# A graph and expert network on one core: the three expert layers split the 626 node columns as 250 + 376, and the steps that use the routing come one up product later

## The reference

```python
xf = layernorm(x)                                   # 625 x 768
probs = softmax(xf @ gate_w.T)                      # 625 x 8 experts
top_w, top_i = top_k(probs, 2)
top_w = top_w / (top_w.sum(-1) + 1e-9)
combine = zeros(625, 8); combine[t, top_i] += top_w
h = gelu(einsum('td,edh->teh', xf, w1) + b1)        # 8 experts of 192 (f0, f3) or 128 (f1)
y = einsum('teh,ehd->ted', h, w2) + b2
x = x + einsum('ted,te->td', y, combine)
```

## Time and profile before

| | |
|---|---|
| three runs | 1741.81, 1742.04, 1739.98 us; median 1741.81 |
| the profiled execution | 1739.98 us; its span from first to last instruction 1740.0 us |
| PE busy | 1682.7 us (97%), 10227 matmuls |
| DVE, POOL, ACT busy | 54%, 40%, 27% of the span |
| chain of work that ended last | PE 82%, DVE 11%, ACT 4% |
| f0: first router matmul, cT transposes | 258.85 us, 279.44 us |
| f1: the same | 514.22 us, 535.98 us |
| f3: the same | 1598.73 us, 1620.90 us |

### The profile page before, as it was taken

How to read it: one execution, slowest core, us unless ns; L and a number is a source line. 1 busy time by engine, 2 the same in 40 slices (tenths; PEclk the granted TensorE clock), 3 DMA queues, 4 the chain that set the end, 5 groups by cost and what they waited for, 6 DMA issues and landing times.

```text
span 1740.0 us, 25810 instructions
## 1 busy us (share of the span) xinstructions
PE 1682.7 (97%) x10227; PEld 1579.9 (91%) x10227; DVE 931.1 (54%) x1879; ACT 466.8 (27%) x875; POOL 690.3 (40%) x428
## 2 busy tenths in 40 slices
PE   8799999999999988899999999999999999999999
PEld 7699999997999988799377888989999999998999
DVE  8993537416866679857497554423112141225731
ACT  6443123203223138934222211101011011112310
POOL 1026865652445520060020175431644435342663
PEclk9899999999999999899899999999999999999999
DMA  2002222423212210014010022111221111110222
GB/s 90 1 28 70 73 69 65 142 78 128 64 55 64 64 56 10 1 47 143 7 43 1 11 85 64 57 45 37 73 64 55 46 51 59 55 55 30 64 73 72
DMA packets 42000, 99.84 MB, mean 57 GB/s; under 512 B 10509, under 2 KB 12143, under 8 KB 41895
## 3 DMA queue, kind: packets, MB, share of 16 engines
q1 hardware_dynamic: 37828, 87.87, 16.3%
q10 hardware_dynamic: 4066, 10.46, 1.7%
HBM read 96.39 MB, written 1.92 MB: 57 GB/s over the span
## 4 chain that ended last, share of the span: by engine, by line
PE 82%; DVE 11%; ACT 4%; issue 1%; POOL 1%; DVEq 0%; POOLq 0%; ACTq 0%
PE bank L2421 10%; PE bank L2423 10%; PE bank L2422 10%; PE banks L2421 9%; PE banks L2422 9%; PE banks L2423 9%; PE bank L2983 3%; PE banks L2983 3%; PE bank L3060 3%; PE bank L3065 3%; PE banks L3060 2%; PE banks L3065 2%; DVE tmp L1827 1%; DVE src_hot L1491 1%; PE banks L2835 1%
## 5 line engine op out<-in xcount | busy, mean ns | idle before, releaser
L833 POOL TENSOR_TENSOR w_hi<-raw,ones_r 128x768 fp32r<-128x768 f32 (+1 forms) x192 | 294.0, 1532 | 994.9 <-PE banks L2423 368.3
L836 POOL TENSOR_TENSOR w_lo<-raw,w_hi 128x768 fp32r<-128x768 f32 (+1 forms) x192 | 370.5, 1930 | 15.0
L2421 PE MATMUL bank<-w_hi,xT_hi 128*125 128x384 f32 (+2 forms) x560 | 187.8, 335 | 1.7 <-DVE small L1968 1.2
L2423 PE MATMUL bank<-w_hi,xT_lo 128*125 128x384 f32 (+2 forms) x560 | 186.7, 333 | 0.0
L2422 PE MATMUL bank<-w_lo,xT_hi 128*125 128x384 f32 (+2 forms) x560 | 186.5, 333 | 0.0
L2421 PE MATMUL banks<-w_hi,xT_hi 128*125 128x384 f32 (+2 forms) x440 | 151.8, 345 | 0.2 <-DVE xT_lo L1569 0.2
L2422 PE MATMUL banks<-w_lo,xT_hi 128*125 128x384 f32 (+2 forms) x440 | 151.4, 344 | 0.0
L2423 PE MATMUL banks<-w_hi,xT_lo 128*125 128x384 f32 (+2 forms) x440 | 151.3, 344 | 0.0
L1618 DVE TENSOR_TENSOR hT_lo<-tmp,hT_hi 128x312 fp32r<-128x312 f32 (+1 forms) x88 | 94.3, 1078 | 41.9 <-ACT hT_hi L970 41.5
L2421 PEld LDWEIGHTS bank<-w_hi,xT_hi 128*125 128x125 f32 x560 | 103.9, 186 | 5.0 <-DVE small L1968 1.4
L2422 PEld LDWEIGHTS bank<-w_lo,xT_hi 128*125 128x125 f32 x560 | 103.9, 185 | 2.5
(11 more groups left out here) (579 smaller groups left out, 3923.4 us busy)
## 6 DMA issues: line engine op xcount, KB each, us to landing
raw<-wa SPq DMA_DIRECT2D x92, 384.0 KB, 3.0
raw<-wc SPq DMA_DIRECT2D x76, 384.0 KB, 3.0
raw<-wb SPq DMA_DIRECT2D x28, 448.0 KB, 3.3
w_rows<-w_in ACTq DMA_DIRECT2D x1, 3072.0 KB, 12.6
bias<-bias_in ACTq DMA_DIRECT2D x6, 384.0 KB
w_first<-w_in ACTq DMA_DIRECT2D x1, 2304.0 KB, 11.2
w_down<-w_down_in SPq DMA_DIRECT2D x8, 288.0 KB, 5.2
w_up<-w_up_in SPq DMA_DIRECT2D x1, 2304.0 KB, 10.6
```

Source lines behind the costliest of these rows:

```text
L833: pool.tensor_tensor(w_hi[:, k, 0:width], raw[:, k, 0:width], ones[:, 0:1].to_broadcast([P, width]), ALU.mult).then_inc(S("unit_high"), 1)
L836: pool.tensor_tensor(w_lo[:, k, 0:width], raw[:, k, 0:width], f(w_hi[:, k, 0:width]), ALU.subtract).then_inc(S("unit_split"), 1)
L2421: tell_used(pe.matmul(dst, l_hi, r_hi, start=start, stop=False))
L2423: return pe.matmul(dst, l_lo, r_hi, start=False, stop=stop)
```

## The change

The expert layers get column parts of their own, 250 (tiles 0 and 1) and 376 (tiles 2 to 4 and the pad). `router(0)` waits for the first two tiles only. The last tile's turn moves behind job 0, `router(1)` behind job 1, the router's transposes behind job 2, the importance of f1 behind job 5, the wait for `combine` with the transposes of the experts' weights behind job 6, and the spreading starts behind job 7. The first four jobs change their order from (unit, part) = (0,0) (0,1) (1,0) (1,1) to (0,0) (1,0) (0,1) (1,1). The slots of `tmp` are five of 376 columns in the same memory, plus two in memory that is free at that time, so seven in all. The down products wait for at least four `low`. The order of the bank plan (`plan_groups`) follows the same steps.

```diff
+EXPERT_CH = [(0, 2 * TN), (2 * TN, NP - 2 * TN)]
...
-EXPERT_LAG = 6
-IMPORTANCE = 3
+EXPERT_LAG = 7
+IMPORTANCE = 5
+EXPERT_SLOTS = 7
+ROUTER_JOB = 1
...
     if s == "g0" and j < 6:
         return j % 3, j // 3
+    if s != "g0" and j < 4:
+        return j % 2, j // 2
     return j // 2, j % 2
+
+
+def columns_of(s, c):
+
+    return (CH if s == "g0" else EXPERT_CH)[c]
...
         add(f + "_routerT", 0, f + "_routerT_read", 1)
-        left_turn()
         jobs, lag = 2 * tiles, EXPERT_LAG
         for j, spread in enumerate(spread_after(jobs)):
             if j < jobs:
                 add(f + "_hidden", j, f + "_activated", j + 1)
             if j == 0:
+                left_turn()
+            if j == ROUTER_JOB:
                 add(f + "_routerT", 1, f + "_routerT_read", 2)
-            if j == 1:
+            if j == ROUTER_JOB + 1:
                 add(f + "_router", 0, f + "_routed", 1)
...
+        last_slots = {s: [at_(f"{s}_slot{i}", [P, EXPERT_CH[1][1]], f32, off)
+                          for i, off in enumerate((XT + up32(KD * NP * 4), HT + 8 * NP * 4 if s == "f1" else NM + 20480))]
+                      for s in ("f0", "f1", "f3")}
...
+        expert_tmp = at_("expert_tmp", [P, TSLOTS - 1, EXPERT_CH[1][1]], f32, tmp_off)
...
+        def slot_of(s, j, cn):
+
+            if s == "g0":
+                return tmp[:, j % TSLOTS, 0:cn]
+            k = j % EXPERT_SLOTS
+            return expert_tmp[:, k, 0:cn] if k < TSLOTS - 1 else last_slots[s][k - TSLOTS + 1][:, 0:cn]
...
                 def router(c):
-                    c0, cn = CH[c]
-                    pe.wait_ge(*E(s + "_xT_low", (6, 2 * NT)[c]))
+                    c0, cn = EXPERT_CH[c]
+                    pe.wait_ge(*E(s + "_xT_low", (4, 2 * NT)[c]))
...
                 router(0)
-                turn_behind(s)(NT - 1)
                 jobs = 2 * tiles
                 for j, spread in enumerate(spread_after(jobs)):
                     if j < jobs:
                         up(s, j)
                     if j == 0:
+                        turn_behind(s)(NT - 1)
+                    if j == ROUTER_JOB:
                         router(1)
-                    if j == 1:
+                    if j == ROUTER_JOB + 1:
                         pe.wait_ge(*E(s + "_routerT_read", 2))
...
-                down(s + "d", s + "_down", hT_hi, hT_lo, lambda k: pe.wait_ge(*E(s + "_low", 2 * k + 2)), seed=seed,
+                down(s + "d", s + "_down", hT_hi, hT_lo, lambda k: pe.wait_ge(*E(s + "_low", max(2 * k + 2, 4))), seed=seed,
```

More of the change, by code:

```diff
@@ L593, in network @@
         tmp = at_("tmp", [P, TSLOTS, WIDE], f32, tmp_off)
+        expert_tmp = at_("expert_tmp", [P, TSLOTS - 1, EXPERT_CH[1][1]], f32, tmp_off)
+        assert (TSLOTS - 1) * EXPERT_CH[1][1] <= TSLOTS * WIDE
         iota = new("iota", [TN, NP], i16)
@@ L962, in hidden @@
                 weighted = full == s + "_weighted"
+                slots = EXPERT_SLOTS if weighted else TSLOTS
                 steps = spread_after(jobs) if weighted else [range(max(j - TSLOTS + 1, 0), max(j - TSLOTS + 2, 0))
@@ L967, in high @@
                     m, c = job_of(s, i)
-                    c0, cn = CH[c]
+                    c0, cn = columns_of(s, c)
                     act.wait_ge(*E(full, i + 1))
-                    act.activation(hT_hi[:, m, c0:c0 + cn], tmp[:, i % TSLOTS, 0:cn], ACT.Copy
+                    act.activation(hT_hi[:, m, c0:c0 + cn], slot_of(s, i, cn), ACT.Copy
                                    ).then_inc(S(s + "_high"), 1)
@@ L976, in hidden @@
                         m, c = job_of(s, j)
-                        cn = CH[c][1]
-                        if made <= j - TSLOTS:
+                        cn = columns_of(s, c)[1]
+                        if made <= j - slots:
                             high(made)
@@ L981, in hidden @@
                         await_group(act, s + "_hidden", j)
-                        if j >= TSLOTS:
-                            act.wait_ge(*E(s + "_low", j - TSLOTS + 1))
-                        act.activation(tmp[:, j % TSLOTS, 0:cn], bank(s + "_hidden", j)[:, 0:cn], func,
+                        if j >= slots:
+                            act.wait_ge(*E(s + "_low", j - slots + 1))
+                        act.activation(slot_of(s, j, cn), bank(s + "_hidden", j)[:, 0:cn], func,
                                        **scale_bias(m)).then_inc(S(s + "_activated"), 1)
@@ L992, in expert_layer @@
                 normal_rows(s)
-                for c, (c0, cn) in enumerate(CH):
+                for c, (c0, cn) in enumerate(EXPERT_CH):
                     await_group(act, s + "_routerT", c)
@@ L1607, in hidden_low @@
                     if j < jobs and weigh:
-                        cn = CH[j % 2][1]
+                        cn = columns_of(s, job_of(s, j)[1])[1]
                         dve.wait_ge(*E(s + "_activated", j + 1))
                         await_group(dve, s + "_cB", j)
-                        TT(tmp[:, j % TSLOTS, 0:cn], tmp[:, j % TSLOTS, 0:cn], bank(s + "_cB", j)[:, 0:cn], ALU.mult
+                        TT(slot_of(s, j, cn), slot_of(s, j, cn), bank(s + "_cB", j)[:, 0:cn], ALU.mult
                            ).then_inc(S(s + "_weighted"), 1)
@@ L1615, in hidden_low @@
                         m, c = job_of(s, i)
-                        c0, cn = CH[c]
+                        c0, cn = columns_of(s, c)
                         dve.wait_ge(*E(s + "_high", i + 1))
-                        TT(hT_lo[:, m, c0:c0 + cn], tmp[:, i % TSLOTS, 0:cn], f(hT_hi[:, m, c0:c0 + cn]),
+                        TT(hT_lo[:, m, c0:c0 + cn], slot_of(s, i, cn), f(hT_hi[:, m, c0:c0 + cn]),
                            ALU.subtract).then_inc(S(s + "_low"), 1)
@@ L2613, in expert_layer @@
                     for i in spread:
-                        m, (c0, cn) = i // 2, CH[i % 2]
+                        m, c = job_of(s, i)
+                        c0, cn = columns_of(s, c)
                         q, kind = (m // 3, m % 3) if tiles == 12 else (m // 2, 2 * (m % 2))
```

## The result

The changed kernel takes 1747.74 us (median of 6 runs, 1746.93 to 1749.9), the kernel before beside it 1742.13 (6 runs): a ratio of 1.0034, 95% interval 1.0024 to 1.0044, so 0.34% slower. The forecast was 1743.7 with a range up to 1747.5; it is missed by 4.0 us, and the range by 0.2.

The account below looks back on a forecast made before the run. PE, busy 97% of the span, was taken as the bound. Earlier router starts (-5.8 us) against new routing stalls (+2.5, +2.7, +2.5) gave +1.9 us on the median 1741.81: 1743.7 us, range 1738.5 to 1747.5.

Parts of the forecast that it names:

- The widths: Expert-layer matmuls: 250 columns cost 0.116 to 0.117 us, 376 cost 0.172, together as before; value 0, +-1.2 us.
- no penalty for narrow ones: Rival for the expert matmuls: narrow ones run at the plain float32 form's rate, +190 us, about 1930 us; chance 0.04.
- The handover: First router matmul starts earlier, f3's last turn waits 0.5 us; gains f0 1.0, f1 0.85, f3 4.0, sum 5.8 us.
- The routing chain: DVE's routing, slowed by POOL, makes PE wait at the experts' weights: 2.5 us in f0 and f3, 2.7 in f1.
- R + 12.8: DVE's chain in f0 and f3 ends 12.8 us after the job behind the router's transposes starts; PE comes at 10.4.
- both comparisons are held: In DVE's routing, POOL delays two comparisons, to 5.3 and 7.2 us after the job behind the router's transposes starts.
- Sum: Net of gains and stalls in the three expert layers: f0 +1.5, f1 +1.85, f3 -1.5, together +1.9 us.
- I count the clock as kept: At f3's router, idle shrinks from 2.7 to 0.5 us, so the lower clock goes away: 1.6 us gained.
- The stalls bring the lower clock: Rival: one to three clock falls behind the new stalls, 1.6 us each, giving 1745.3 to 1748.6 us; chance 0.24.
- idle there with a fall of the clock behind it: Sign of being wrong: PE idle at the experts' weight transposes (L2608), followed by the lower clock.
- the matmuls around the stalls are dense: Argument against clock falls at the new stalls: matmuls there are dense, those before f3's router were short transposes.
- 2.1 us of cover: One more job before PE asks for combine; four jobs, 10.4 us, still lie between in f0, as before.

Follow-up runs that it names:

- e1: Changed kernel, but POOL starts the second weight unit given back behind the router's numbers only after the copies into cpad, in all three expert layers; 1738.7 us, 0.9978 of before.
- e3: Changed kernel, but PE fills its wait for cpad in each expert layer with 14 thrown-away products of 376 columns; 1743.34 us, 1.0011 of before.
- e9: Changed kernel with lag 8 and eight slots, plus ten thrown-away products (1.7 us) ahead of f1's transposes of the experts' weights; 1733.84 us, 0.9959 of before.
- e12: Changed kernel with lag 8 and eight slots, plus five thrown-away products (0.9 us) ahead of f1's transposes of the experts' weights; 1737.61 us, 0.9966 of before.
- e8: Changed kernel with the lag left at 6 and six slots, so new parts and order alone; 1742.90 us, 1.0005 of before.
- e11: Changed kernel (lag 7), but POOL holds back only the third weight unit until cpad is made; 1737.99 us, 0.9973 of before.
- e10: Changed kernel with lag 6, six slots, importance behind up product 4, and POOL holding the second weight unit until cpad is made; 1737.76 us, 0.9976 of before.
- e2: Changed kernel with every step that uses the routing one up product later (lag 8, eight slots); 1737.3 us, 0.9974 of before.
- e4: Changed kernel with even column parts (312 and 314) again and the first router product waiting for six copies as before; 1755.83 us, 1.0082 of before.

## Why the prediction was wrong

**What held.** The widths: products of 250 columns start 0.117 us apart and of 376 columns 0.172 to 0.173, together what 312 and 314 cost; no penalty for narrow ones. The handover: no idle time at the router, 0.53 us for the last turn in f3. The routing chain: four POOL instructions back to back and two more from R + 8.7, the chain's end at R + 12.8, stalls of 2.31, 2.55 and 2.25 us where 2.5, 2.7 and 2.5 were forecast, with one slip inside: the second comparison was not held, the add behind it was, and that the sum came out all the same is luck. e1 shows the cause by taking it away. Here the rule of the Trainium skill that was weighed in the prediction (page "SBUF — State Buffer", section "Who interferes with whom") says that a DVE instruction with two SBUF inputs contends with a GpSimd instruction that reads SBUF. The trace agrees: the first comparison takes 1.41 us beside POOL and the add 1.78, in place of 0.20. The prediction took from it that both comparisons are held; L1671 was not, at 0.19 us in the gap between two of POOL's.

**The step that failed.** It is in the paragraph "Sum": the three new stalls stand in it at their length alone (2.5, 2.7, 2.5), with nothing for the clock behind them. "I count the clock as kept" held where it was said, at f3's router (the granted clock is 1.00 from 1601.6 to 1608.0, where before had 0.73), but a new fall came behind f3's stall and another behind f1's. By its own terms: f0 +1.5 forecast, +1.2 measured; f1 +1.85, +3.1; f3 -1.5, +0.05. The misses of f1 and f3 (1.25 and 1.55 us) are the 1.4 and 1.5 us that came off when e3 filled the wait. The case stood among the rivals, "The stalls bring the lower clock" (two falls at its 1.6 us make 1746.9), and had 0.24; "idle there with a fall of the clock behind it" was also the prediction's own sign of being wrong. What spoke against it there, that the matmuls around the stalls are dense, did not save it: in f1 and f3 the clock fell in both profiles of the changed kernel. That it did not fall in f0 in either could have been read from nothing shown before.

**The rest, 1.6 us of the span** (+2.2, -0.8 and +0.2 in three stages). The prediction took the stages it doesn't touch as fixed. They are not: between f1 and f3 the trace took 984.2 to 990.2 us over fourteen profiles of twelve kernels with the same instructions there. In the changed kernel that stage was 2.3 us longer than before on the mean of two profiles each, 1.3 of it by one fall of the clock behind an idle time of 1.9 us that before has as well. e9's profile, with the work behind f1 shifted by 1.7 us, does not have that fall; e12's, with 0.9 us, has it. With the times listed there a mere shift is the likely reason, though argued and not shown, since the clock of one kernel also differs from execution to execution. What decides it at a given time is not settled by these runs, nor is the rest of the 2.3 us, which lies in more falls between 680 and 740 us of the traces.

**The lag.** The prediction priced the later consumer as 2.1 us of cover that the longer first products used up. It worked out rightly that the third unit comes back at R + 8.3 and lies beside the chain, but not that the old lag would have kept it away; e8, e11 and e10 show that this was the change's own doing. In one series the kernel took 1747.0 us with lag 7 and 1742.9 with lag 6, and 2.9 of these 4.1 us lie in the three layers (206.7 against 203.8): 0.7 of idle time in each of f0 and f3, and the fall of the clock behind f3's.

**A version that beats both.** The new parts and order with lag 8 (e2, 1737.3 us), or with lag 6 and POOL held (e10, 1737.8), are 0.24 to 0.26% faster than before. About 6.4 us come off the three layers by the table (202.4 to 196.0), and some of it is given back in the untouched stage. e9's 1733.8 is at best a lucky shift in time and no design.

## What to carry to other kernels

When work on an engine is moved behind one more step to give a chain time, ask what that step releases on other engines: here the product that was to cover the chain also set POOL going beside it, and the two together cost more than the old lag. A small-vector chain on DVE should be priced with POOL's schedule beside it, and keeping POOL off it by one wait (e1, e11) can be worth more than a longer lag. On a PE-bound kernel a new idle time of 2 us should be priced at its length plus a fall of the clock, as the more likely case and not as a remote one (at the transposes of the experts' weights the clock fell behind eight of the ten waits of 2.0 to 2.6 us in these profiles), and stages that are merely shifted in time have an uncertainty of their own, 2 to 3 us here.

## What was not expected of the hardware

- The clock fell behind idle times of PE of 1.9 to 2.6 us in some places and not in others, and behind the same idle time in one kernel and not in another: 2.31 us in f0 without a fall (changed, both profiles), 2.07 us there with one (e4), 1.88 and 1.89 us in attention with and without. Behind 1.57 us (e8, f0 and f3) it did not fall. One fall costs 1.3 to 1.5 us. The Trainium skill, page "TensorE: Matmul & The Clock Gate", section "Why this matters for your kernels", advises against idle gaps between bursts of matmuls, but only against longer ones than any of these. The trace agrees in kind; the clock fell behind shorter gaps, though, and the length of the gap alone did not decide it.
- Between POOL's `w_hi` and `w_lo` there is a gap of about 0.07 us (273.01 + 1.47 = 274.48 to 274.55), and in the changed kernel the second comparison got through in it at full speed (L1671, 0.19 us; in f1 and f3 as well). It had been free to start, since it does not wait for the instruction ahead of it. The CAST of L1694, which waits for L1692, started at 279.50, 0.01 us behind `w_lo`, and took 1.83 us. Of the routing's 125x40 TENSOR_TENSORs that started beside one of POOL's instructions, and not in such a gap, none of 132 in the fourteen profiles took under 1.1 us.
- With 1.7 us of wasted matmuls ahead of it a stage of unchanged instructions took 984.2 us in place of 989.3 (e9, e2), and where it got shorter the granted clock was higher. The medians differ by 3.5 us, but on five runs their intervals overlap.
